# Combination weights of three mixture-of-experts layers: how they are stored in DRAM and how the experts' loads read them

## The reference

```
L0: probs = softmax(x @ Wg.T);  keep the top 4 of 16;  combine[t, e] = prob or 0
    h = silu(x @ W1[e].T) * (x @ W3[e].T)            # 16 experts of width 176
    out = sum_e (h * combine[:, e]) @ W2[e].T  + shared   # shared: width 352, weight 1
L2: route = sigmoid(x @ router_w); the top 1 of 8;  8 experts of width 512
L3: softmax with bias, the top 4 of 16, renormalised; 16 experts of width 224
x = x + tanh(g_ffn[l]) * out
```

## Time and profile before

| what | value |
|---|---|
| median of three runs | 3038.99 us |
| the profiled execution, and its span | 3039.76 us, 3038.0 us |
| mean granted TensorE clock | 0.873 |
| busy share PE / PEld / DVE / ACT / POOL | 86 / 62 / 55 / 35 / 29 % |
| experts, L0 / L2 / L3: first load to end of stage | 387.9 to 594.1 / 1920.6 to 2177.9 / 2811.6 to 3032.8 us |
| DMA queue of SP | 264.79 MB, 32.3% of 16 engines |

### The profile page before, as it was taken

One profiled execution on the slowest core, in us unless ns is written; L12 is line 12 of the kernel. 1 busy time (PEld: TensorE's weight loads), 2 busy tenths in 40 slices (PEclk: granted clock), 3 DMA queues, 4 the chain that ended last, 5 costly groups with the idle time before them and its releaser, 6 DMA issues. The chain is left out here.

```text
span 3038.0 us, 35920 instructions
## 1 busy us (share of the span) xinstructions
PE 2621.5 (86%) x11837; PEld 1878.6 (62%) x11837; DVE 1675.4 (55%) x2714; ACT 1067.5 (35%) x1602; POOL 875.8 (29%) x533
## 2 busy tenths in 40 slices
PE   7776379789999996897999998799779999995898
PEld 4775379755555554663555555699755555554897
DVE  4453234427767664586767673344337677663444
ACT  3222034323444441212444442344323444440443
POOL 0222023102343440262434342133102344340232
PEclk8555689878999998797999999799768999997999
DMA  1233044533433412024343330233443333310443
GB/s 41 88 118 121 10 109 116 155 113 97 99 78 86 94 48 86 17 73 117 86 97 84 81 74 7 86 123 112 137 137 90 86 90 88 84 43 8 117 115 95
DMA packets 106476, 266.27 MB, mean 88 GB/s; under 512 B 23755, under 2 KB 55157, under 8 KB 105048
## 3 DMA queue, kind: packets, MB, share of 16 engines
q1 hardware_dynamic: 106360, 264.79, 32.3%
HBM read 221.62 MB, written 42.96 MB: 87 GB/s over the span
## 5 line engine op out<-in xcount | busy, mean ns | idle before, releaser
L1072 DVE TENSOR_REDUCE att_top<-banks 128x1 f32<-128x500 f32 x1008 | 643.2, 674 | 347.4 <-PE banks L1013 345.1
L1130 ACT ACTIVATE att_ex<-banks 125x896 f32<-125x896 f32 x576 | 526.5, 918 | 363.3 <-PE banks L1000 363.3
L1179 POOL TENSOR_TENSOR att_acc<-att_acc,att_two 125x896 f32<-125x896 f32 x186 | 392.0, 2107 | 463.7 <-DVE att_two L1087 450.0
L1401 PE MATMUL banks<-moe_xs,moe_w 128*128 128x448 f32 x2040 | 446.3, 369 | 70.3 <-DVE moe_xs L1516 68.0
L1013 PE MATMUL banks<-att_kh,att_q 128*128 128x500 f32 x1008 | 399.6, 448 | 98.7 <-DVE att_top L1072 44.4
L1028 PE MATMUL banks<-att_ex,att_v 125*64 125x448 f32 x2304 | 466.9, 547 | 0.0
L1401 PEld LDWEIGHTS banks<-moe_xs,moe_w 128*128 128x128 f32 x2040 | 387.1, 190 | 103.7 <-DVE moe_xs L1516 69.4
L1484 POOL TENSOR_TENSOR moe_sc<-moe_sg,moe_cb 128x448 f32<-128x448 f32 x170 | 196.1, 1153 | 705.3 <-ACT moe_sg L1458 705.3
L1000 PE MATMUL banks<-att_q,att_kh 128*125 128x448 f32 x1152 | 353.8, 389 | 2.2 <-ACT att_ex L1130 2.2
L1013 PEld LDWEIGHTS banks<-att_kh,att_q 128*128 128x128 f32 x1008 | 203.1, 203 | 230.4 <-DVE att_top L1072 133.4
L1087 DVE TENSOR_TENSOR att_two<-att_ex 125x896 f32<-125x896 f32 x288 | 317.9, 1142 | 49.9 <-ACT att_ex L1130 49.5
(11 more groups left out here) (184 smaller groups left out, 2348.8 us busy)
## 6 DMA issues: line engine op xcount, KB each, us to landing
moe_cb<-comb_rows SPq DMA_DIRECT2D x85, 448.0 KB
att_kh<-kvt_hi SPq DMA_DIRECT2D x96, 375.0 KB, 6.9
moe_raw<-L_experts_dram SPq DMA_DIRECT2D x85, 384.0 KB, 6.2
q_rows<-mats_q SPq DMA_DIRECT2D x24, 896.0 KB
att_q<-q_rows SPq DMA_DIRECT2D x48, 448.0 KB, 7.4
att_kl<-kvt_lo SPq DMA_DIRECT2D x48, 375.0 KB, 4.8
att_v<-kvn SPq DMA_DIRECT2D x24, 750.0 KB
att_qm<-q_rows SPq DMA_DIRECT2D x48, 224.0 KB, 3.4
```

The costliest lines, as they stand in the source:

```text
L1072: dve.tensor_reduce(top[:, s % 2, n // NS, n % NS:n % NS + 1], PS[6 + (PIECES * s + n) % 2][:, 0:SB], AX.X, ALU.max).then_inc(mx_done, 1)
L1130: act.activation(ex[:, u % RING], scored, ACT.Exp).then_inc(exp_done, 1)
L1179: pool.tensor_tensor(a, two[:, 0] if n == 1 else a, two[:, n % 3], ALU.add).then_inc(gathered, 1)
L1401: last = pe.matmul(PS[2 * e + m][:, 0:HALF], w[:, s, pw, o:o + 128], xs[:, px, k, HALF * e:HALF * e + HALF], start=n == 0, stop=n == 3 * K ...
```

## The change

`comb_rows` has 19 rows instead of 209. `route` stores each row of combT once, in two transfers (rows 0 to 15 and 16 to 18 in L0, 0 to 3 and 4 to 7 in L2, 0 to 7 and 8 to 15 in L3), and waits for both. `experts` loads `moe_cb` by two transfers for each chunk: partitions 0 to `cut` from the row of the first group's expert, the others from the row of the last group's expert. Where a chunk lies within one expert, the cut is at 64 and both read the same row. Which row and which cut is worked out in Python, so SP's stream is no longer a hardware loop: all chunks are written out. The order of SP's waits and loads stays. GpSimd waits for 32 instead of 16 for each chunk.

```diff
-def route(nc, G, l, E, top, kind, rows, groups_per_expert):
+def route(nc, G, l, E, top, kind, rows):
...
                 sp.wait_ge(tr_copied, 2)
-                sp.dma_start(G["comb"][0:rows * groups_per_expert, :].rearrange("(e g) n -> e g n", e=rows),
-                             combT[:, :].unsqueeze(1).broadcast_to([rows, groups_per_expert, T])).then_inc(stored, 16)
-                sp.wait_ge(stored, 16)
+                halves = ((0, E), (E, rows)) if rows > E else ((0, E // 2), (E // 2, E))
+                for a, z in halves:
+                    sp.dma_start(G["comb"][a:z, :], combT[a:z, :]).then_inc(stored, 16)
+                sp.wait_ge(stored, 32)
...
-def experts(nc, G, l, chunks, group_rows, W):
+def experts(nc, G, l, chunks, group_rows, groups_per_expert, W):
...
-                def chunk(i, s, first, more):
-                    c = 2 * i + s
-                    if not isinstance(i, int) or i:
+                def weights_of(c, s):
+
+                    of = [(c * groups + g) // groups_per_expert for g in range(groups)]
+                    cut = of.count(of[0]) * group_rows
+                    cut = cut if cut < 128 else 64
+                    for e, a, z in ((of[0], 0, cut), (of[-1], cut, 128)):
+                        sp.dma_start(cb[a:z, s, :], G["comb"][e:e + 1, :].broadcast_to([z - a, T])).then_inc(cb_in[s], 16)
+
+                for c in range(chunks):
+                    s = c % 2
+                    if c >= 2:
                         sp.wait_ge(d_split, c - 1)
-                    sp.dma_start(raw[:, s, :], w_dram[bass.ds(c * 128, 128), :]).then_inc(w_in[s], 16)
-                    if not isinstance(i, int) or i:
+                    sp.dma_start(raw[:, s, :], w_dram[c * 128:c * 128 + 128, :]).then_inc(w_in[s], 16)
+                    if c >= 2:
                         sp.wait_ge(comb_done, 2 * c - 2)
-                    sp.dma_start(cb[:, s, :], G["comb"][bass.ds(c * groups, groups), :].unsqueeze(1)
-                                 .broadcast_to([groups, group_rows, T])).then_inc(cb_in[s], 16)
-
-                emit(sp, chunk)
+                    weights_of(c, s)
...
-                    pool.wait_ge(cb_in[s], i * 16 + 16)
+                    pool.wait_ge(cb_in[s], i * 32 + 32)
...
-        G["comb"] = nc.dram_tensor("comb_rows", [19 * 11, T], FP32, kind="Internal").ap()
+        G["comb"] = nc.dram_tensor("comb_rows", [19, T], FP32, kind="Internal").ap()
```

More of the change, by code:

```diff
@@ L1650, in feed_forward @@
         group_rows = np.gcd(width, 128).item()
-        route(nc, G, l, E, top, kind, rows, width // group_rows)
-        experts(nc, G, l, CHUNKS[l], group_rows, W)
+        route(nc, G, l, E, top, kind, rows)
+        experts(nc, G, l, CHUNKS[l], group_rows, width // group_rows, W)
 def attention(nc, G, l):
```

## The result

The changed kernel took 2997.8 us in the median (4 runs, 2990.52 to 3001.24), the kernel before 3039.32 us: ratio 0.9867, 95% interval 0.9842 to 0.9892. The profiled execution took 2990.52 us, its span 2988.7 us (3038.0 before).

A forecast was written before the change was run, and what follows sets the result against it. It took SP's store wait to set the end of routing and TensorE to bound the experts' loop. Store -33.3, start +0.4 and end +0.9 gave -32.0 us, so 3007.0 us, range 3001 to 3014.

The forecast's parts named there:

- the main term: Routing stages of L0, L2 and L3: the smaller comb_rows store shortens SP's waits, saving 33.3 us.
- The store: End of the routing stages: three store stretches of 40.5 us in all shrink to 2.4 us each, saving 33.3 us.
- the small store: Attention's 3.5 KB store, taken as nearest measured row: 0.343 us of issue and 1.07 us of wait, 1.4 together.
- the 0.6 counted for the rows: Part of each new 2.4 us store stretch: 0.6 us for moving the rows, from 0.6 to 0.7 us a row.
- The start of the experts: Chunk 0's raw reaching ScalarE: L0 and L3 take L2's value, +0.4 us, bounds 0 and +1.0.
- The end: Experts of L0 and L2: second cb issue delays fold weights, +0.9 us; bounds +1.5 and -1.5.
- The loop: Experts' loop: 85 cb loads become 170, raw lands in some 4 to 5 us, no gain and no loss.
- The three terms of changed stages: Routing store -33.3 us, start of the experts +0.4, end of the experts +0.9: -32.0 us in sum.
- I count 0, at either sign: Granted clock after the shorter store waits: TensorE starts from the same level as before, so 0 us.
- Hence no gain and no loss in the loop: TensorE hides it: Experts' loop: new cb loads and slightly later raw stay covered by TensorE's 7.3 us a chunk, 0 us.
- My bounds of 26 to 37 us: Bounds of the total saving, 25.7 to 36.6 us, summed over store, start and end of the experts.
- about 1 us on each side for the scatter: Whole kernel: allowance for scatter of medians, widening 3002.4 to 3013.3 to the range 3001 to 3014 us.

The follow-up runs named there:

- copies_many_engines: Kernel before with only L0's store changed: the same 209 copies in two transfers, rows 0 to 15 and 16 to 18; 3015.5 us, ratio 0.9934.
- one_store: Changed kernel with each layer's compact rows stored in one transfer instead of two; 2997.8 us.
- two_cb: Changed kernel with every cb transfer made twice, the extra ones into spare tiles; 3004.0 us, ratio 0.9893, two executions.
- four_cb: Changed kernel with every cb transfer made four times, the extra ones into spare tiles; 3246.1 us, ratio 1.069, two executions.
- one_load: Changed kernel with one cb transfer of 128 partitions where a chunk lies within one expert, two otherwise; 2991.2 us, ratio 0.984.
- early_fold: Changed kernel with one cb transfer for single-expert chunks, chunk 0's raw loaded alone, and fold weights spread over the loop; 2985.3 us, ratio 0.9834.
- big_tensor: Changed kernel with comb_rows allocated at 209 rows as before, 19 used, so later DRAM tensors keep their addresses; 2997.0 us, ratio 0.9857.
- loads_only: Kernel before with only the experts' loads changed and SP's loop written out, the old store kept; 3032.0 us, ratio 0.999.

## Why the prediction was wrong

The direction, the place and the mechanism of the main term were right, the sum too small: 32.0 forecast, 41.5 measured, 40.0 +- 2.2 in the pooled means.

- **The store.** 33.3 us forecast, 34.6 measured: the new stretches are 1.9 to 2.0 us, not 2.4. A pair of plain issues takes 0.6 us and not 0.7, and the wait behind it is 1.3 us, only 0.3 above the 1.07 of the small store, so most of the 0.6 counted for the rows does not appear. The reading of the windows (one engine, 26 GB/s) was borne out by copies_many_engines and one_store.
- **The start of the experts.** +0.4 forecast, +1.9 measured. L2, which I had taken as the model and counted at 0, lost 0.8 itself. Over the six profiles with the old loads and the ten with both halves (two_cb, four_cb, one_load and early_fold left out) the start changes by +0.1 in L0, +0.7 in L2 and +0.8 in L3; in L2 it is the second issue (one_load), in L3 it stays open.
- **The end.** +0.9 forecast, -1.6 measured. In L0 the bound became the value, -1.5 us, which fits its reason (a cb transfer that was uneven over the engines had delayed the last one), though no run took this apart. In L2 the pair shows -0.1; over the same six and ten profiles it is -1.2 +- 0.5 in L0 and +0.5 +- 0.7 in L2, where 0.45 was counted. The experts' stages as a whole give +1.7; 0.5 of this is L3's first 12 matmuls, which ran longer at the lower clock (4.86 us for 4.39).
- **The loop.** No gain and no loss within it: right, with the landings forecast (4 to 5 us, measured 4.2).
- **The step that failed.** The three terms of changed stages, -32.0 forecast, measured -32.7 in the first pair, with errors that cancel in part; there the total was lucky. What failed is "I count 0, at either sign" for the clock, with "Hence no gain and no loss in the loop: TensorE hides it" for the loads. I took stages with unchanged code as constant. Six of them are 6.8 +- 3.2 us shorter in the kernels with the new loads, where TensorE spends less time at the lower level. Part of it may be waits: PE's two main waits in the three attention stages, for VectorE's reduce and for att_q, sum to 86.8 us before and 83.2 after, 3.6 of the 10.7 us by which these stages differ in the first pair. My bounds of 26 to 37 us held only the terms of changed stages, and they left out 40. The "about 1 us on each side for the scatter" was mis-sized as well: single executions of one kernel scatter with a standard deviation of 5.1 us, so a median of four is uncertain by some 5 us, more than the 3 us by which the result missed the range; and the three runs that the forecast started from stood 2.5 us above the pooled mean of before.

What stays open is how loads in one stage come to change the clock in the next. The two halves of the change are told apart, addresses are excluded (big_tensor and loads_only have those of before), position found no support, but which property of the new loads does it (their 16 engines, their two issues, the end of L0's stage) was not tried. With the scatter of 5 us between executions, it would take as many runs for each. That there is such an effect at all rests on one profile for each run, and stages ahead of every change differ between the two groups by 1.2 +- 1.1 us too.

## What to carry to other kernels

A store of a few partitions behind which a barrier stands is read first by its DMA share: 0.06 of 16 engines says that one engine works, and the cure is the outermost dimension (16 + 3 for 19) as much as the number of bytes. Loads that repeat rows can be given the same outermost dimension: with it the transfer queued behind them landed after 4.2 us in place of 6.2 and 8.1. In this kernel that gained nothing in the loop, since TensorE hid it. And a forecast for one place of a 3 ms program needs the scatter of all the others in its range: here single executions of one kernel spread over 24 us, more than half the gain.

## What the runs showed of the hardware beyond that

- The queries' stage of L1 took about 69.3, 71.0, 71.8 or 72.6 to 73.3 us in the 20 profiles, with 32, 38, 38 and 42 us of it at the lower clock: few values, not a spread. Two kernels with the same code there, or two executions of one kernel, may differ by 4 us from the clock alone.
- The matmuls of the experts' loop come every 202 to 203 ns in most stages and every 206 to 207 ns in some, a whole stage long, at the same granted clock of 1.00 and with no wait. L2's loop in two executions of the kernel before:
```profile
1930.00:2140.00 210.00, 209.24 (x1028) 193.54 (x1027) 97.88 (x171) 91.01 (x172) 65.91 (x58) 1.00 0.36 115
```
```profile
1930.00:2140.00 210.00, 209.25 (x1013) 189.75 (x1012) 97.94 (x171) 89.98 (x171) 65.34 (x57) 1.00 0.36 114
```
  The amount of DMA does not decide it (115 and 114 GB/s here, and two_cb's 178 GB/s in L0 went with 202.3 ns). Of the three loops of the 19 profiles without four_cb, 12 of 57 have the longer spacing: 1 of 18 with the old loads, 11 of 39 with the new, two of these in early_fold. 4 ns over the 1152 matmuls of L2's loop are some 5 us. What decides is open.
- Issuing a store of 19, 8 or 16 whole rows takes SP 0.24 to 0.32 us, and the repeated rows took 0.69 to 0.86.
